# Gate and up projections of a fused attention and gated-MLP layer by seven block products instead of eight

## The chip, the cores and the metric

The kernel runs on one core of one Trainium2 chip. Its time is what the device takes for one launch, in microseconds (us); the three runs of the kernel before took 1195.88 to 1196.09 us, with a median of 1195.92 us. PE is TensorE (matrix products), DVE is VectorE, ACT is ScalarE, POOL is GpSimd, and SP is the engine whose queue issues the DMA transfers.

## The reference

The layer normalises 2 x 1024 tokens of width 512, runs a causal linear attention with 16 heads, adds its normalised output to the input, and then runs a gated MLP whose hidden values are thinned out: of each four neighbours only the two largest in magnitude stay.

```python
x = x + _layernorm(attention(_layernorm(x), Wq, Wk, Wv, Wo))
x = x + _layernorm(ffn(_layernorm(x), w_gate, w_up, w_down))

def ffn(x, w_gate, w_up, w_down):          # x: (2, 1024, 512)
    h = silu(x @ w_gate) * (x @ w_up)      # 512 -> 2048, twice
    h_sparse = _sparsify_2to4(h)           # keep 2 of each 4 neighbours
    return h_sparse @ w_down               # 2048 -> 512
```

Everything is float32. The kernel reaches that precision by splitting each operand into a high part (rounded to the matmul's fp32r type) and a low part (the rest). Each product then takes three matmuls: high x high, low x high, high x low.

## The kernel before

All five engines run programs written out by hand, which meet at semaphores. Each engine works strictly in its own program order. Time is cut into slots. 66 attention slots (`slot_a`, 0 to 65) come first and then 76 MLP slots (`slot_f`, 0 to 75). `TICKS` (L37) gives the common order, and every engine has its own `slot_a` and `slot_f`.

The MLP works on eight units (`UNITS`: two batches times four blocks of 512 hidden values), each with eight slots. A unit has two halves of 512 tokens, and a half has four row blocks (i = 0 to 3) of 128 hidden values, ordered so that the four blocks hold the four neighbours of each group. In slot n PE runs, for one row block and one half of the tokens:

- `gate(n)`: four 128-wide slices of the input (KT = 4), three matmuls each, 12 in all, into a gate bank (`psG`);
- `down(y)`: 12 matmuls of the down projection for 128 tokens of an earlier half;
- `project(psU..)`: 12 matmuls of the up projection into an up bank (`psU`).

Two gate banks and two up banks are used in turn, so that PE fills one while ACT and DVE empty the other. ACT computes silu straight from the gate bank (L1001), DVE multiplies it with the up bank into `hid` (L1255), and ACT writes the magnitudes (L997). After four slots DVE compares pairs (`pair`, L1206), makes the masks and multiplies (`keep_two`, L1212), ACT casts the high parts (L1006) and POOL and DVE subtract to get the low parts (L1401 through the helper at L1339, and L1239). DVE adds each finished `down` bank to `Y` (L1271). DVE also has the statistics of the normalisations (`variance`, L1057, three instructions), POOL the power and the shift (L1344, L1357) and ACT the scaling (L936).

Weights come in pieces of 128 x 512 through a ring of four staging buffers. ACT casts the high part (L891), and POOL subtracts the low part (L1339). A gate or up piece is loaded once per unit and serves both halves, so a unit takes eight such pieces and four pieces of the down weights.

The normalised input of the MLP is turned by PE (`turn`, L601), and split by ACT (`split_x`, L852) and DVE (L1081) into `Xh`, `Xl`, which hold both batches' halves: batch 1 is turned in slots 8 to 22 (`MID_1`, L84), long before slot 32 needs it. The last unit's second half is masked after the last gate product, next to nine remaining `down`s.

Of the kernel before, what the change touches and what calls it, by code (L numbers as in the profile page):

```python
# [7 lines left out]
ALU = mybir.AluOpType  # L8
# [5 lines left out]
P = 128  # L14
B, S, DM = 2, 1024, 512
KVH, REP = 4, 4
W = 512
# [8 lines left out]
LAST = SLOTS - 8  # L26
OPEN = 13
# [21 lines left out]
def down_at(n):  # L49
    y = n - 6 if n < 60 else 54 if n == 61 else n - 9 if n >= SLOTS else -1  # L50
    return y if 0 <= y < SLOTS else None


# [29 lines left out]
MID_0 = [39, 42, 43, 46, 47, 50, 51, 54]  # L83
MID_1 = [8, 10, 12, 14, 16, 18, 20, 22]  # L84


def sum_tick(kind, b, t):
    if kind == "res":
        return tick_a(32 * b + 26 + t)
    return tick_f(65 + t if b else 30 + t)  # L90
# [8 lines left out]
def stat_tick(job):  # L99
    if job[0] in ("res", "out"):  # L100
        return sum_tick(*job)
    return turn_tick(*job) - 2


def norm_tick(job):
    if job[0] in ("res", "out"):
        return sum_tick(*job) + 1
    return turn_tick(*job) - 1
# [18 lines left out]
def weight_plan():  # L127
    plan = [(("q", 0, i), -1) for i in range(4)] + [(("k", 0, 0), -1)]
    plan += [(("v", 0, kk), -1) for kk in range(KT)] + [(("o", 0, h), -1) for h in range(4)]
    for u in range(1, UNITS + 1):  # L130
# [4 lines left out]
        else:  # L135
            plan += [(("g", 0, 0), base - 1), (("g", 0, 1), base)]
        if u > 1:
            plan += [(("o", u - 1, h), base + 1) for h in range(4)]
        if more:
# [4 lines left out]
            if u == NU:  # L144
                plan += [(("v", 1, 2), base + 4), (("v", 1, 3), base + 5)]
    plan += [(("g", 0, 2), 58), (("g", 0, 3), 59), (("u", 0, 0), 60), (("u", 0, 1), 61), (("u", 0, 2), 64),
             (("u", 0, 3), 65)]
    for u in range(UNITS):
        plan += [(("d", u, i), tick_f(8 * u + 1 + i)) for i in range(3)]
        down = [(("d", u, 3), tick_f(8 * u + 5 if u else 4))]  # L150
        if u in (0, UNITS - 1):
            plan += down
        if u + 1 < UNITS:
            for j in range(4):
                plan += [(("g", u + 1, j), tick_f(8 * u + 5 + j)), (("u", u + 1, j), tick_f(8 * u + 5 + j))]
                if j == 0 and u:
                    plan += down
# [7 lines left out]
def by_dve(piece):  # L165
    return piece[0] == "d" and piece[2] == 3


def split_count(k):
    kind = by_dve(PLAN[k][0])  # L170
    return sum(by_dve(piece) == kind for piece, _ in PLAN[:k + 1])


def pieces_at(tick, kinds):
    return [k for k, (piece, when) in enumerate(PLAN) if when == tick and piece[0] in kinds]
# [15 lines left out]
def build(nc, x, wq, wk, wv, wo, wg, wu, wd, cos_t, sin_t, causal, eye, x1, v_rest, out):  # L191
    with ExitStack() as ctx:
        def sb(name, shape, dtype=F32):
            return ctx.enter_context(nc.sbuf_tensor(name, shape, dtype))
# [5 lines left out]
        with ExitStack() as early:  # L200
# [1277 lines left out]
```

## Time and profile before

| | |
|---|---|
| median of three runs | 1195.92 us (1195.88 to 1196.09) |
| profiled execution, first to last instruction | 1194.3 us |
| outside that span (median less span) | 1.6 us |
| PE busy | 1183.0 us, 99% |
| DVE busy | 762.5 us, 64% |
| ACT busy | 497.5 us, 42% |
| POOL busy | 493.6 us, 41% |

The page names no time of its own for the profiled execution beside its span, so the span stands for it. The busy time of an engine is the union of its instructions. PE's matmuls are pipelined: each is shown as some 0.39 us, but a new one starts about every 0.227 us, and that distance, not the shown length, is what a matmul costs. DVE's instructions overlap a little too, so that the distance from one start to the next is again the better measure.

### The profile page before, as it was taken

What the parts mean: (1) busy time and instruction counts of PE and PEld (TensorE: products, weight loads), DVE (VectorE), ACT (ScalarE), POOL (GpSimd) and SP (SyncE); (2) the same over time, 40 slices, a digit from 0 to 9 for tenths busy, and PEclk for the clock granted to TensorE, in tenths of its full rate; (3) what the DMA queues carried; (4) which work ended last, traced back from release to release, by engine and by line L of the source; (5) the groups of instructions that cost most, each with busy time, mean ns of one, the idle gap of its engine ahead of it and who ended that gap; (6) DMA issues with size and microseconds to landing.
All of it is one profiled execution on the core that took longest, in us unless ns stands there. A gap on an engine that the chain in (4) does not pass through costs nothing.

```text
span 1194.3 us, 16009 instructions
## 1 busy us (share of the span) xinstructions
PE 1183.0 (99%) x5958; PEld 998.5 (84%) x5958; DVE 762.5 (64%) x1300; ACT 497.5 (42%) x981; POOL 493.6 (41%) x399
## 2 busy tenths in 40 slices
PE   9999999999999999999999999999999999999997
PEld 7888888888888888888888888888888888888885
DVE  8944756756664456666665476676567765555568
ACT  5534444544544345455355443433333342333322
POOL 6421533515555125244245444443425552334313
PEclk9999999999999999999999999999999999999998
DMA  7221323323534214133143222211103231212111
GB/s 225 80 78 52 102 72 80 89 49 80 146 98 141 58 47 131 47 87 94 30 124 102 97 80 71 71 62 45 62 12 105 97 98 45 62 44 62 45 44 71
DMA packets 58222, 95.03 MB, mean 80 GB/s; under 512 B 6944, under 2 KB 15392, under 8 KB 58144
## 3 DMA queue, kind: packets, MB, share of 16 engines
q1 hardware_dynamic: 58144, 94.01, 27.2%
q8 instruction: 47, 0.77, 0.3%
q14 instruction: 31, 0.25, 0.1%
HBM read 67.24 MB, written 11.53 MB: 66 GB/s over the span
## 4 chain that ended last, share of the span: by engine, by line
PE 95%; DVE 3%; DMA 0%; issue 0%; POOL 0%; ACT 0%; SPq 0%; DVEq 0%
PE bank_q L567 10%; PE bank_q L565 10%; PE bank_q L566 10%; PE bank_y L567 5%; PE bank_y L566 5%; PE bank_y L565 5%; PE bank_od L724 5%; PE bank_od L565 4%; PE bank_od L566 4%; PE bank_od L567 4%; PE bank_od L727 4%; PE bank_t L567 4%; PE bank_t L565 4%; PE bank_t L566 4%; PE bank_s L565 4%; PE bank_s L566 4%
## 5 line engine op out<-in xcount | busy, mean ns | idle before, releaser
L565 PE MATMUL bank_q<-x_hi,w_hi 128*128 128x512 f32 x432 | 172.9, 400 | 0.0
L1339 POOL TENSOR_TENSOR w_lo<-stage,w_hi 128x512 fp32r<-128x512 f32 x80 | 109.3, 1376 | 147.9 <-ACT w_hi L891 147.2
L567 PE MATMUL bank_q<-x_lo,w_hi 128*128 128x512 f32 x432 | 168.9, 391 | 0.0
L566 PE MATMUL bank_q<-x_hi,w_lo 128*128 128x512 f32 x432 | 168.3, 390 | 0.0
L1339 POOL TENSOR_TENSOR big_lo<-hidden,big_hi 128x512 fp32r<-128x512 f32 x30 | 69.0, 2321 | 188.5 <-ACT big_hi L1006 188.5
L1339 POOL TENSOR_TENSOR big_lo<-q_rows,big_hi 128x1024 fp32r<-128x1024 f32 x31 | 74.0, 2386 | 117.2 <-ACT big_hi L930 117.2
L997 ACT ACTIVATE scratch<-hidden 128x512 f32<-128x512 f32 x64 | 40.6, 634 | 176.2 <-DVE hidden L1255 176.2
L567 PE MATMUL bank_y<-wout_lo,a_hi 128*128 128x512 f32 x256 | 100.0, 391 | 0.0
L565 PE MATMUL bank_y<-wout_hi,a_hi 128*128 128x512 f32 x256 | 99.8, 390 | 0.0
L566 PE MATMUL bank_y<-wout_hi,a_lo 128*128 128x512 f32 x256 | 99.8, 390 | 0.0
L567 PEld LDWEIGHTS bank_q<-x_lo,w_hi 128*128 128x128 f32 x432 | 81.1, 188 | 17.6
L724 PE MATMUL bank_od<-v_rows,scratch 128*128 128x130 f32 x512 | 95.2, 275 | 0.0
L566 PEld LDWEIGHTS bank_q<-x_hi,w_lo 128*128 128x128 f32 x432 | 81.3, 188 | 15.4
L565 PEld LDWEIGHTS bank_q<-x_hi,w_hi 128*128 128x128 f32 x432 | 81.2, 188 | 15.3
L959 ACT ACTIVATE scratch<-bank_od,small 128x128 f32<-128x128 f32 x256 | 73.5, 374 | 42.1 <-DVE small L1161 42.1
L727 PE MATMUL bank_od<-st_rows,q_rows 128*128 128x130 f32 x448 | 86.6, 275 | 0.0
L1339 POOL TENSOR_TENSOR wout_lo<-stage,wout_hi 128x512 fp32r<-128x512 f32 x44 | 67.2, 1552 | 42.3 <-ACT wout_hi L891 42.3
L971 ACT CAST a_hi<-bank_s 128x512 fp32r<-128x512 f32 x64 | 37.6, 587 | 111.6 <-PE bank_s L689 111.6
L724 PEld LDWEIGHTS bank_od<-v_rows,scratch 128*128 128x128 f32 x512 | 79.1, 191 | 3.7
L1344 POOL TENSOR_TENSOR small<-small 128x1 f32<-128x1 f32 x64 | 38.0, 593 | 86.4 <-DVE small L1072 85.8
L1271 DVE TENSOR_TENSOR y_acc<-bank_od,y_acc 128x512 f32<-128x512 f32 x42 | 28.8, 685 | 63.7 <-PE bank_od L567 63.7
L727 PEld LDWEIGHTS bank_od<-st_rows,q_rows 128*128 128x128 f32 x448 | 67.5, 190 | 0.0
(333 smaller groups left out, 2987.3 us busy)
## 6 DMA issues: line engine op xcount, KB each, us to landing
q_rows<-scratch SPq DMA_DIRECT2D x116, 128.0 KB, 2.3
x_rows<-x SPq DMA_DIRECT2D x48, 256.0 KB, 2.9
stage<-wq SPq DMA_DIRECT2D x32, 256.0 KB, 2.7
stage<-wo SPq DMA_DIRECT2D x32, 256.0 KB, 2.7
stage<-wg SPq DMA_DIRECT2D x32, 256.0 KB, 2.6
stage<-wu SPq DMA_DIRECT2D x32, 256.0 KB, 2.8
stage<-wd SPq DMA_DIRECT2D x32, 256.0 KB, 2.6
x<-x_rows SPq DMA_DIRECT2D x16, 256.0 KB, 2.4
```

What stands on the lines that cost most here:

```text
L565: pe.matmul(ps, whi, xhi, start=first, stop=False, skip_group_check=True)
L566: pe.matmul(ps, wlo, xhi, start=False, stop=False, skip_group_check=True)
L567: return pe.matmul(ps, whi, xlo, start=False, stop=last, skip_group_check=True)
L724: ins = pe.matmul(o, Sf[:, h * P:(h + 1) * P], Vr[:, c, :], start=True, stop=first, skip_group_check=True)
L727: ins = pe.matmul(o, Q[:, (2 * p + h // 2) % 4, h % 2, t], St[:, :], start=False, stop=True, skip_group_check=True)
L959: act.activation(Tn[:, h * P:(h + 1) * P], sums[:, h // 2, h % 2, 0:P], ACT.Identity, scale=share[:, h:h + 1]).then_inc(act_a, 1)
L971: copy(Ah[:, :, :].rearrange("p h t -> p (h t)"), psS[:, :]).then_inc(act_ah, 1)
L997: act.activation(ab[:, i, :], hid[:, i, :], ACT.Abs).then_inc(act_ab, 1)
L1271: dve.tensor_tensor(Y[:, t, :], down_bank(y), Y[:, t, :], ALU.add).then_inc(dve_yf, 1)
L1339: return pool.tensor_tensor(dst, full, hi.bitcast(F32), ALU.subtract)
L1344: pool.tensor_tensor(rstd[q % 4], mv[q % 4][:, 1:2], mhalf, ALU.pow).then_inc(pool_rs, 1)
```

## The change

Strassen's scheme computes a 2 x 2 block product with seven block products instead of eight. Here the blocks are two row blocks of the weights, two halves of the input width (KT = 4 slices become two and two), and two halves of the tokens. A group of four slots, a quad (`quad_of`), now makes two row blocks for both halves of the tokens, where before it made four row blocks for one half. Its seven products are made for gate and for up, 14 in all of six matmuls each (84 matmuls, where four slots of `gate` and `project` had 96).

- **PE.** The quad's four beats are `products_12`, `products_67`, `products_5`, `products_34`. There is one pair of banks (gX, uX, which collect a running sum) and another (gY, uY). A sum in gX or uX is copied out by ACT before PE adds the next product to it, and DVE adds gY or uY to the copies.
- **Row sums.** ACT: six copies a quad (`keep_sums`) and four silus. DVE: three `gate_sum`, three `up_sum`, four `gated`.
- **Weights.** The products need sums and differences of weight blocks: `combine_weights` on DVE, twice a quad with four instructions of 128 x 256. Seven pieces (`unit`) a quad are split by ACT and POOL, where before it was eight in two quads. They stand in a ring of five. Two of the seven are split as two halves.
- **Input.** For tokens 512 to 1023 of a batch, DVE makes the combinations T1, T2, T3 (`combine_x`, six instructions of 128 x 256) and T4 (`combine_4`, three of 128 x 1024); ACT and POOL split them (`cast_t`, `t_low`, `cast_t4`, `t4_low`). There is room for one batch's combinations alone, so batch 1 is turned in slots 29 to 32 (`MID_1`), split in slots 30 to 33 (`SPLIT_1`), and its T4 is made in slot 34. Batch 0's are made in attention slots 55 to 62.
- **Masks.** Both halves of a unit's tokens are complete only when its second quad is, so the masking comes later (slots 8u + 8 to 8u + 13), and so do the `down`s (`down_beat`). Twelve `down`s stand behind the last product, where nine did.

The core of the diff, with most of the semaphores, buffers and bookkeeping left out:

```diff
+def down_beat(y):
+    if y >= LAST:
+        return y + 9
+    v, j = y // 8, y % 8
+    n = 8 * v + 11 + min(j, 6)
+    if v == 2 and 3 <= j <= 5:
+        return 32
+    return SLOTS if y > 51 else n
-MID_1 = [8, 10, 12, 14, 16, 18, 20, 22]
+MID_1 = [29, 29, 30, 31, 31, 32, 32, 32]
+STAT_1 = [27, 27, 28, 30, 30, 31, 32, 32]
+NORM_1 = [28, 28, 29, 31, 31, 32, 32, 32]
+SPLIT_1 = [30, 30, 31, 32, 32, 32, 33, 33]
+            def product(ps, v, side, of, first):
+                wh, wl = w_hi[:, v % RING, HALVES[side]], w_lo[:, v % RING, HALVES[side]]
+                for kk in range(2):
+                    c = slice(kk * P, kk * P + P)
+                    ins = three(ps, wh[:, c], wl[:, c], of[0][:, kk, :], of[1][:, kk, :], first and kk == 0, kk == 1)
+                return ins
+            def products_12(k):
+                g.wait_ge(dve_xl, 4 * (5 + 2 * b))
...
+                product(gX, v, 0, B11, True).then_inc(pe_g, 1)
...
+                product(gY, v, 1, B21, True).then_inc(pe_g, 1)
...
+                product(uX, v + 1, 0, B11, True).then_inc(pe_u, 1)
...
+                product(uY, v + 1, 1, B21, True).then_inc(pe_u, 1)
+            def products_67(k):
+                g.wait_ge(pool_tl, 4 * (b + 1))
...
+                product(gX, v + 2, 0, T2, False).then_inc(pe_g, 1)
+                g.wait_ge(dve_cg, 3 * k + 1)
+                product(gY, v + 2, 1, T3, True)
...
+            def products_34(k):
...
+                g.wait_ge(act_n, 6 * k + 5)
+                product(gX, v + 5, 0, B22, False).then_inc(pe_g, 1)
+                g.wait_ge(dve_cg, 3 * k + 2)
+                g.wait_ge(pool_t4, b + 1)
+                product(gY, v + 5, 1, T4, False).then_inc(pe_g, 1)
...
+            def keep_sums(k, i):
...
+                copy(gates[(0, 2, 1)[i]], gX).then_inc(act_n, 1)
...
+                copy(hid(u, row, h), uX).then_inc(act_n, 1)
+            def combine_weights(k, up):
...
+                g.wait_ge(pool_w, 7 * k + 3 if up else 7 * k - 1)
+                dve.tensor_tensor(one, c1, c2, ALU.add).then_inc(dve_ss, 1)
+                dve.tensor_tensor(three, a1, c1, ALU.subtract)
+                g.wait_ge(dve_ss, own + 1)
+                dve.tensor_tensor(two, one, a1, ALU.subtract).then_inc(dve_ss, 1)
+                g.wait_ge(dve_ss, own + 2)
+                dve.tensor_tensor(four, a2, two, ALU.subtract).then_inc(dve_ws, 1)
+            def combine_4(b):
...
+                dve.tensor_tensor(to, B21[0].bitcast(F32), T2[0].bitcast(F32), ALU.subtract).then_inc(dve_t4s, 1)
+                dve.tensor_tensor(to, to, B21[1].bitcast(F32), ALU.add).then_inc(dve_t4s, 1)
+                dve.tensor_tensor(to, to, T2[1].bitcast(F32), ALU.subtract).then_inc(dve_t4, 1)
+            def gate_sum(k, i):
...
+                dve.tensor_tensor(to, to, gY, ALU.add).then_inc(dve_cg, 1)
 # DVE, slot_f
+                for t in splits:
+                    if t != 5:
+                        split_x(("mid", 1, t))
+                for job in stats:
+                    if job[0] == "mid":
+                        variance(job)
+                if n < SLOTS and beat == 0:
+                    if u and not second_half:
+                        pair(u - 1, 1, 0)
+                    elif u:
+                        keep_masks(u - 1, 1)
+                    gate_sum(k, 0)
...
+                    up_sum(k, 0)
...
+                    if u and not second_half:
+                        keep_masks(u - 1, 0)
+                if n < SLOTS and beat == 2:
+                    gate_sum(k, 1)
+                    for y in downs:
+                        add_down(y)
+                    up_sum(k, 1)
+                    if k + 1 < QUADS:
+                        combine_weights(k + 1, 0)
+                    if second_half:
+                        pair(u, 0, 0)
+                if n < SLOTS and beat == 3:
+                    gated(k, 1)
+                    for y in downs:
+                        add_down(y)
+                    if u and not second_half:
+                        pair(u - 1, 1, 1)
+                    gate_sum(k, 2)
+                    gated(k, 2)
+                    up_sum(k, 2)
+                    if k + 1 < QUADS:
+                        combine_weights(k + 1, 1)
...
+                if n == 34:
+                    combine_4(1)
+                for w in range(UNITS):
+                    if n == late_piece(w):
+                        split_down(w)
```

## Rows read from the trace of the kernel before

**Rows 1.** The page: busy time, share of the span, instructions.
```profile
PE 1183.0 (99%) x5958; PEld 998.5 (84%) x5958; DVE 762.5 (64%) x1300; ACT 497.5 (42%) x981; POOL 493.6 (41%) x399
```
**Rows 2.** The page: the chain that ended last, by engine.
```profile
PE 95%; DVE 3%; DMA 0%; issue 0%; POOL 0%; ACT 0%; SPq 0%; DVEq 0%
```
**Rows 3.** PE's timeline, slot 1: start us, us, engine, line, operation, tiles.
```profile
669.35 0.39 PE L565 MATMUL bank_q<-x_hi,w_hi 128*128 128x512 f32 x1
...
672.07 0.39 PE L565 MATMUL bank_q<-x_hi,k_hi 128*128 128x512 f32 x1
```
**Rows 4.** DVE's timeline, one half of the tokens in slots 28 to 32.
```profile
909.10 0.69 DVE L1208 TENSOR_TENSOR scratch<-scratch 128x512 bf16<-128x512 f32 x1 [0.70 <-ACT scratch L997]
909.71 0.68 DVE L1209 TENSOR_TENSOR scratch<-scratch 128x512 f32<-128x512 f32 x1
...
911.03 0.69 DVE L1215 TENSOR_TENSOR scratch<-scratch 128x512 bf16<-128x512 f32 x1
...
914.30 0.68 DVE L1227 TENSOR_TENSOR hidden<-hidden,scratch 128x512 f32<-128x512 f32 x1
914.90 0.42 DVE L1229 TENSOR_TENSOR scratch<-scratch 128x512 bf16<-128x512 bf16 x1
915.24 0.42 DVE L1231 TENSOR_TENSOR scratch<-scratch 128x512 bf16<-128x512 bf16 x1
...
917.55 3.33 DVE L1239 TENSOR_TENSOR big_lo<-hidden,big_hi 128x512 fp32r<-128x512 f32 x2
```
**Rows 5.** Groups by line, whole trace: busy us, mean ns, idle before.
```profile
L1239 DVE TENSOR_TENSOR x_lo<-hidden,x_hi 128x512 fp32r<-128x512 f32 x4 | 2.5, 684 | 0.0
L1157 DVE TENSOR_SCALAR small<-bank_od 128x4 f32<-128x4 f32 x64 | 10.0, 157 | 65.4 <-PE bank_od L727 59.8 <-PE bank_od L724 5.5
L1068 DVE BATCH_NORM_STATS2 small<-x_rows 128x6 f32<-128x512 f32 x24 | 16.4, 684 | 0.1
L1321 DVE TENSOR_TENSOR big_lo<-q_rows,big_hi 128x1024 fp32r<-128x1024 f32 x1 | 1.2, 1218 | 0.0
L1344 POOL TENSOR_TENSOR small<-small 128x1 f32<-128x1 f32 x64 | 38.0, 593 | 86.4 <-DVE small L1072 85.8
L1339 POOL TENSOR_TENSOR big_lo<-q_rows,big_hi 128x1024 fp32r<-128x1024 f32 x31 | 74.0, 2386 | 117.2 <-ACT big_hi L930 117.2
```
**Rows 6.** POOL's timeline, slots 22 to 26.
```profile
856.63 1.30 POOL L1339 TENSOR_TENSOR u_lo<-stage,u_hi 128x512 fp32r<-128x512 f32 x1
883.01 4.60 POOL L1339 TENSOR_TENSOR big_lo<-hidden,big_hi 128x512 fp32r<-128x512 f32 x2 [19.14 <-ACT big_hi L1006]
```
**Rows 7.** DVE's and POOL's timelines over the same five microseconds.
```profile
932.92 1.00 DVE L1208 TENSOR_TENSOR scratch<-scratch 128x512 bf16<-128x512 f32 x1
933.85 1.77 DVE L1209 TENSOR_TENSOR scratch<-scratch 128x512 f32<-128x512 f32 x1
933.33 1.74 POOL L1339 TENSOR_TENSOR wout_lo<-stage,wout_hi 128x512 fp32r<-128x512 f32 x1
```
**Rows 8.** ACT's groups, 700 to 1140 us.
```profile
L997 ACT ACTIVATE scratch<-hidden 128x512 f32<-128x512 f32 x54 | 34.2, 634 | 156.5 <-DVE hidden L1255 156.5
L891 ACT CAST w_hi<-stage 128x512 fp32r<-128x512 f32 x32 | 19.0, 613 | 0.0
L936 ACT ACTIVATE x_rows<-x_rows,small 128x512 f32<-128x512 f32 x8 | 6.5, 816 | 4.3 <-POOL small L1357 4.3
```
**Rows 9.** DVE's timeline in attention slot 61.
```profile
641.48 0.69 DVE L1189 TENSOR_TENSOR y_acc<-bank_y,y_acc 128x512 f32<-128x512 f32 x1 [2.06 <-PE bank_y L567]
```
**Rows 10.** The end: DVE's timeline, and the granted clock by windows (PEclk after the busy times).
```profile
1161.23 0.69 DVE L1255 TENSOR_TENSOR hidden<-bank_t,scratch 128x512 f32<-128x512 f32 x1 [2.95 <-PE bank_t L567]
1186.04 0.68 DVE L1271 TENSOR_TENSOR y_acc<-bank_od,y_acc 128x512 f32<-128x512 f32 x1
1187.00:1188.00 1.00, 0.00 (x0) 0.00 (x0) 0.90 (x4) 0.94 (x2) 0.80 (x3) 1.00 0.66 248
1188.00:1189.00 1.00, 0.00 (x0) 0.00 (x0) 1.00 (x3) 0.69 (x1) 0.78 (x1) 0.62 0.00 0
```

More of the change, by code:

```diff
@@ L26 @@
 LAST = SLOTS - 8
+QUADS = SLOTS // 4
+RING = 5
 OPEN = 13
@@ L941, in slot_a @@
                 m = s - 1
+                late = []
                 if s % 4:
@@ new lines, in slot_f @@
+                for job in norms:
+                    if job[0] == "mid":
+                        normalise(job)
+                if n < SLOTS and beat == 0:
+                    if not second_half and u:
+                        absolute(u - 1, 1, 0)
+                    keep_sums(k, 0)
+                    silu(k, 0)
+                    if 5 in splits:
+                        split_x(("mid", 1, 5))
+                    unit(7 * k + 5)
+                    unit(7 * k + 6)
+                    if second_half:
+                        absolute(u, 0, 1)
@@ L1083, in split_x @@
                 half, t = halves(*job), job[2] % 4
+                if job[0] == "mid" and job[2] > 3:
+                    combine_x(job)
+                    return
+                if job[0] == "mid":
+                    half = 0
                 g.wait_ge(act_xh, k + 1)
@@ new lines, in slot_a, with pair @@
+                if s == 61:
+                    combine_4(0)
+                if s == 62:
+                    combine_weights(0, 1)
+            def pair(u, i, h):
+                low, high, c = (least_23, most_23, c23) if i else (least[h], most[h], c01[h])
+                r = pair_number(u, i, h)
+                g.wait_ge(act_ab, r + 1)
+                dve.tensor_tensor(c, low, second, ALU.is_ge)
+                dve.tensor_tensor(high, low, second, ALU.max)
+                dve.tensor_tensor(low, low, second, ALU.min).then_inc(dve_pr, 1)
@@ L1272, in slot_f @@
-                for job in at(tick, stat_tick, LATER + ENDING):
-                    variance(job)
-                for k in pieces_at(tick, "d"):
-                    if by_dve(PLAN[k][0]):
-                        split(k)
+                k, beat = quad_of(n)
+                u, second_half = k // 2, k % 2
+                splits = [t for t in range(TT) if SPLIT_1[t] == n]
+                downs = [y for y in range(SLOTS) if add_beat(y) == n]
+                stats = at(tick, stat_tick, LATER + ENDING)
```

763 lines of the change are left out of this document (544 added, 219 removed).

## The prediction

> **What bounds the kernel now.** First the busy times: PE is busy for 99% of the span, DVE for 64%, the others for 41 to 42% [rows 1]. Then the chain that ended last: 95% of it is PE [rows 2]. So a matmul taken away is worth its whole distance to the next one, as long as PE is kept fed. That distance is in PE's timeline: twelve matmuls lie between 669.35 and 672.07 us, 0.227 us each [rows 3]. What the change loads instead is DVE, and DVE's own pace is read from starts. A 128x512 fp32 instruction follows the one before it after 0.60 us (909.10 to 909.71), a bf16 one after 0.34 (914.90 to 915.24), and the mask work from L1215 up to the first product takes 3.3 us, with the two bf16 instructions behind it 4.0 [rows 4]. A low part costs 0.68 us alone [rows 5], but two of them take 3.33 us while POOL works on its own low parts [rows 4, 6].
>
> **What the change takes away.** Four slots had 96 gate and up matmuls, a quad has 84. Over 16 quads 192 are gone: 192 x 0.227 = 43.5 us. Downs, turns and the attention keep their counts. If nothing else moved, the span would be 1194.3 - 43.5 = 1150.8.
>
> **What it adds in a steady pair of quads.** PE now needs 264 x 0.227 = 59.8 us for two quads (65.4 before). DVE, at 0.60 an instruction and 0.33 for one of 128x256 (my estimate, halfway from a 128x4 one at 0.16 to the 0.60; bounds 0.16 and 0.60) [rows 4, 5]: 12 sums and 8 products 12.0, pairs 12 x 0.60 = 7.2, masks 2 x 4.0 = 8.0, masked products 4.8, low parts 2.4 undisturbed, 8 downs 4.8, sixteen half-wide weight combinations 5.3, one weight split 0.6. That is 45.1 of 59.8 us, 75%; before it was 32.6 of 65.4. So on average PE still sets the pace. But DVE's work is one queue, and PE's next product waits at fixed places in it.
>
> I walked two quads beat by beat with these numbers, PE's beats being 36, 48, 12, 36, 36, 36, 24 and 36 matmuls. ACT copies (0.61 each [rows 8]) and sums come in time nearly everywhere: a bank filled in one beat is wanted again a beat later, some 5 us on. The weak place is the short third beat (12 matmuls, 2.7 us, no down) of a unit. There DVE has the sum, two downs, the sum, `combine_weights` and then `split_down`, which waits for ACT; and ACT gets to it only after three weight units, two magnitudes and two casts (about 4 us at 0.61 to 0.63 [rows 8]). Behind the waiting split stand `gated`, `pair` and the third `gate_sum`. That sum ends about 10 us after the fourth beat began, while PE wants it 9.5 us after (36 + 6 matmuls): 0.4 us late undisturbed, 3 us with the disturbance below. I take 2 us at each of six such places, 12 us (bounds 2 and 24). A seventh lies in the batch change.
>
> **The shared disturbance.** When POOL subtracts from SBUF, DVE's two-input instructions from SBUF stretch: L1209 took 1.77 us, not 0.68, while POOL's own took 1.74, not 1.30 [rows 4, 6, 7]. The two take turns. POOL's steady load rises from 15 subtractions in two quads (8 + 4 + 3) to 21 (14 + 4 + 3), DVE's two-input work from SBUF from about 23 to 32 us. The Trainium skill has this as a rule (SBUF — State Buffer, "SBUF: two separate sides"): the port pair that VectorE and GpSimd share is an exclusive lock for a whole instruction. The trace agrees, with 1.77 and 1.74 us for the two that met. What it would make of the time is the second rival.
>
> **Batch 0's combinations (attention slots 55 to 62).** Added on DVE: four `combine_x` (6 x 0.33 and three short waits, 2.3 us each), one `combine_4` (3 x 1.22 = 3.7 us), two weight combinations (1.3 each). A slot there has about 2 us of idle DVE before it takes PE's output [rows 9], which hides most; `combine_4` alone exceeds it, and two `combine_x` meet in slots 55 and 59. I take 4 us (0 to 10, the sum of 15.5 less six slots' idle, is the outer bound).
>
> **Batch 1's combinations (slots 28 to 35).** Before, the turning lay in slots 8 to 22, far ahead. Now three things come one after another with little for PE to do.
> 1. `products_12(8)` needs the low part of tile 3. Up to there DVE has in slots 30 to 32 three `variance`s at 1.1 (0.68 for the first of their three instructions [rows 5], the two short ones make up the rest: my estimate), four splits of 0.6, seven sums and products 4.2, a down 0.6, a pair 1.8 and two combinations 2.7, 15 us, behind a backlog of some 2.5 (tiles 0 to 2 have their `variance`s in slots 27 and 28), with about 2 us of waits for POOL and ACT. PE has 12 + 24 matmuls and the turns, 9.5 us. ACT's normalisation of tiles 3 and 4 (0.82 each) waits for POOL, which stands behind the unit that waits for DVE's combination. PE starts 10 us late (7 to 11).
> 2. `products_67(8)` needs the T's of tile 7. From the start of slot 32 PE has 24 matmuls, three turns and three downs, 15 us. DVE has a `combine_x`, two `variance`s, a wait for POOL's scalings and ACT's normalisations and magnitudes, a pair, two sums, a `combine_x`, two downs, the masks (4.0) and two more `combine_x`: 23 us, then 1 for ACT and 2 for POOL (1.30 and half of it). PE waits 9.5 us (7 to 13).
> 3. `products_34(8)` needs T4. Its chain starts with the end of the first half of `products_5(8)`: copy 0.8, sum 0.6, two downs 1.2, sum 0.6, weights 1.3, `combine_4` 3.7, ACT about 1.1, POOL 2.4 [rows 5, 8], hand-overs 0.6: 12.3 us. PE has 12 matmuls, 2.7 us. It waits 9.5 us (8 to 12).
> Together 29 us (22 to 36). This is the largest cost, and nothing hides it: PE's program has no other work between these points.
>
> **The clock.** At the end the granted clock was still 1.00 in 1187 to 1188 and 0.62 in 1188 to 1189, with PE's last matmul near 1186 [rows 10]. So it falls to its lower level, 1.2 GHz, some 2 us after work stops. After each of the three long waits PE would begin at half speed. No row shows how long; if it is as long as the fall took, 2 us at half speed lose 1 us. I take 3 us for three waits (0 to 12).
>
> **Results of batch 0 (slots 36 to 43)** add DVE's `variance` (1.1) and POOL's scalings (0.6 and more [rows 5]) and additions to these fuller beats: 3 us (0 to 8).
>
> **The end.** Before, the last product's result came at 1161.2 and the last down's at 1186.0: nine downs (24.5 us) without a gap [rows 10]. Now both halves of the last unit wait for the last product. Four older downs cover 10.9 us; the first masked half needs sum and product 1.5, magnitudes 1.4, pair 1.9, down 0.6, masks 4.0, down 0.6, first product 0.6, ACT 0.8 and POOL up to 2.3, 13.5 us, and the second low part 2 more. PE waits 4.5 us, and about 2.5 for the second half: 7 us (4 to 11).
>
> **Sum.** 1194.3 - 43.5 + 12 (steady) + 4 (attention) + 29 (batch change) + 3 (clock) + 3 (results) + 7 (end) = 1208.8 of span. The median stands 1.6 us above the span, so I forecast 1210.4 us, 1.2% slower. The 58 us of new waits come from bounds of 28 and 101; I trust the middle, since most terms are chains with named instructions.
>
> **Rivals.**
> - *The seams are short (faster).* The mechanism: DVE reaches the batch change with no backlog and 128x256 instructions cost nearer 0.2 than 0.33, so that the chains in 1 and 2 shrink to 6 us each; T4's wait of 8 stays, the steady places cost 2, the end 5, the attention 1. That is 28, and 2 for the clock, against 43.5: 1182 us. For it: DVE is at 75%, and PE never waited in the trace of before. Against it: the work in slots 30 to 33 is counted instruction by instruction. It decides as soon as the waits are under 43.5 us. Chance 0.33.
> - *The pair of engines is the bound (slower still).* If the two engines take turns without exception, as in [rows 7], DVE's 32 us of two-input work and POOL's 21 subtractions at 1.30 (27 us, [rows 6]) fill 59 of the 59.8 us of two quads. Every wait of one for a semaphore is then lost to PE as well; at some 4 us for each of seven pairs of quads (about the 3.5 us by which the two low parts of [rows 4] and POOL's pair of [rows 6] stretch together) that is 28 us beyond the forecast, 1238 us. This is what the Trainium skill's rule (SBUF — State Buffer, "SBUF: two separate sides") would lead to. Against it: in 883.01 to 887.61 POOL did two of 1.3 us while DVE did some 3 us of its own [rows 4, 6], so about a tenth overlaps. Chance 0.14.
> - *It doesn't do what it says:* PE waits as much as it saves and the time stays at 1196. Chance 0.04.
>
> **How the numbers follow.** The forecast (1198.5 to 1222) has 0.49. The range over the cases is 1174 to 1238: it leaves out a tenth on either side. A measurement of this kernel tells 0.2% (2.4 us) from no change. Faster by more than that 0.33, within it 0.04, slower by more 0.63.
>
> **What would show it.** PE: 5766 matmuls (5958 - 192), at 0.227 us where it is fed. PE idle in slots 31 to 35 of the MLP in three gaps of about 10 us, the first ended by DVE's `split_x`, the others by POOL's `t_low` and `t4_low`; the granted clock under 1.00 behind them. DVE busy above 80% of the MLP's span, POOL above 55%. Gaps of a few us at the start of every other quad, ended by `gate_sum`. I am wrong if the MLP shows PE without gaps in slots 28 to 35, or if the gaps before T4 are under 5 us.

## The result, and the profile after

The changed kernel takes 1323.36 us (median of four runs, 1322.28 to 1324.45) against 1196.01 (1195.88 to 1196.15) for the kernel before in the same comparison. The ratio is 1.1065 with an interval of 1.1049 to 1.108. The forecast was 1210.4 with a range of 1174 to 1238: the side is right, the size is far off.

The page of the changed kernel, busy times and three rows of the forty slices, and the chain that ended last:

```profile
PE 1190.7 (90%) x5766; PEld 984.8 (75%) x5766; DVE 985.2 (75%) x1568; ACT 580.9 (44%) x1175; POOL 599.8 (45%) x499
...
PE   9999999999999999999788798987666888998886
...
DVE  8745766666655566667747898997877879898998
...
PEclk9999999999999999999999999998778998999998
...
PE 55%; DVE 29%; issue 6%; ACT 5%; POOL 4%; DMA 0%; DVEq 0%; SPq 0%; ACTq 0%
```

PE has its 192 matmuls fewer (5958 before, [rows 1]), and yet its share falls from 99 to 90% and its part of the chain from 95% [rows 2] to 55%. DVE has 29% of the chain. The two engines' rows show two kinds of loss: PE at 8 and 9 through most of the MLP, and a hole at the batch change.

The waits of PE from the MLP's first sum to the end (line, what it waited for, us in total, times, longest):

```profile
PE bank_t L652 <- DVE scratch L1591: 21.3, 16, 2.2
PE bank_q L652 <- ACT scratch L1189: 15.1, 6, 4.7
PE bank_od L652 <- POOL wout_lo L1775: 12.5, 5, 2.6
PE bank_t L652 <- POOL x_lo L1775: 12.3, 1, 12.3
PE bank_q L652 <- POOL x_lo L1775: 11.8, 1, 11.8
PE bank_od L652 <- DVE y_acc L1619: 7.6, 4, 2.8
```

`gate_sum` (L1591), at the start of the quads, is the largest. The two long waits, for the low parts of T1 to T3 and of T4, stand where they were forecast.

The table splits the loss by stage. A unit runs from its first `gate_sum` to the next unit's. "PE needs" is the count of its matmuls at 2.72 / 12 = 0.227 us (a turn of four short ones at 0.44). "Lost" is the length less that need. The first and last rows are measured against the kernel before. The first `gate_sum` comes at 677.8 us, and PE of the kernel before had done as many matmuls in time for a sum at 658.7. From there on the last unit has 384 matmuls, which with the work behind them take 95.6 us at the pace of the kernel before. The last two columns are two of the experiments below (11 and 14).

| stage | PE needs | length after | lost after | lost, POOL thin | lost, all thin |
|---|---|---|---|---|---|
| attention's end | | | 19.1 | 16.0 | 3.6 |
| unit 0 | 41.0 | 56.2 | 15.2 | 9.2 | 7.3 |
| unit 1 | 51.7 | 67.0 | 15.3 | 3.3 | -0.1 |
| unit 2 | 59.8 | 70.2 | 10.4 | 1.3 | 0.3 |
| unit 3 (turning of batch 1) | 56.6 | 87.5 | 30.9 | 20.7 | 17.4 |
| unit 4 (T's of batch 1) | 66.6 | 105.1 | 38.5 | 28.2 | 14.9 |
| unit 5 | 59.8 | 77.9 | 18.1 | 5.5 | 2.2 |
| unit 6 | 59.8 | 70.2 | 10.4 | 1.2 | 0.3 |
| unit 7 and the end | 95.6 | 108.5 | 12.9 | 2.9 | 3.7 |
| sum | | | 170.8 | 88.3 | 49.6 |

The spans differ by 1320.5 - 1194.3 = 126.2 us, and with the 43.5 saved 169.7 are lost. The rows add up to 1.1 us more, since the matmuls of the kernel before are not exactly 0.2267 us apart in the MLP either (0.2274). The most telling row is unit 2, which has no turning and no statistics, only the steady work: 70.2 us, where the kernel before took 65.4.

What DVE does there is in the timelines. First DVE, then POOL, in a stretch of attention slot 60 where both work on weights:

```profile
641.78 0.42 DVE L1411 TENSOR_TENSOR w_sums<-stage 128x256 f32<-128x256 f32 x1
642.11 1.52 DVE L1412 TENSOR_TENSOR w_sums<-stage 128x256 f32<-128x256 f32 x1
643.55 1.51 DVE L1414 TENSOR_TENSOR w_sums<-w_sums,stage 128x256 f32<-128x256 f32 x1
645.09 1.37 DVE L1416 TENSOR_TENSOR w_sums<-stage,w_sums 128x256 f32<-128x256 f32 x1
```
```profile
641.95 2.83 POOL L1775 TENSOR_TENSOR w_lo<-stage,w_hi 128x512 fp32r<-128x512 f32 x2 [1.92 <-ACT w_hi L1043]
644.74 1.45 POOL L1799 TENSOR_TENSOR x_rows<-x_rows,y_acc 128x512 f32<-128x512 f32 x1
```

The first combination starts before POOL does and takes 0.42 us. The next starts 0.33 us behind it, which is what the prediction estimated. By then POOL has begun, and each further one takes 1.37 to 1.52 us, the length of one POOL instruction: the last two end at 645.06 and 646.46, 0.3 us after POOL's subtractions end at 644.78 and 646.19. Four cost 4.6 us, not 1.3.

### The profile page after: what moved, and what is told of

Read it like the earlier page. It is cut to its first block, busy times and chain, and to the rows that moved or that the text cites. A ratio compares the mean times of both kernels' runs of the same rounds, so it can differ in the third digit from the quotient of the medians.

```text
span 1320.5 us, 16350 instructions
## 1 busy us (share of the span) xinstructions
PE 1190.7 (90%) x5766; PEld 984.8 (75%) x5766; DVE 985.2 (75%) x1568; ACT 580.9 (44%) x1175; POOL 599.8 (45%) x499
## 4 chain that ended last, share of the span: by engine, by line
PE 55%; DVE 29%; issue 6%; ACT 5%; POOL 4%; DMA 0%; DVEq 0%; SPq 0%; ACTq 0%
PE bank_q L652 6%; PE bank_q L654 6%; PE bank_q L653 6%; PE bank_y L654 4%; PE bank_y L652 4%; PE bank_y L653 4%; PE bank_od L869 4%; PE bank_od L872 3%; PE bank_t L652 2%; PE bank_s L776 2%; PE bank_t L654 2%; PE bank_t L653 2%; DVE w_sums L1412 2%; DVE w_sums L1414 2%; DVE scratch L1591 2%
## 5 line engine op out<-in xcount | busy, mean ns | idle before, releaser
L652 PE MATMUL bank_q<-x_hi,w_hi 128*128 128x512 f32 x496 | 206.1, 416 | 39.4 <-ACT scratch L1189 15.1
L653 PE MATMUL bank_q<-x_hi,w_lo 128*128 128x512 f32 x496 | 198.8, 401 | 0.0
L654 PE MATMUL bank_q<-x_lo,w_hi 128*128 128x512 f32 x496 | 198.8, 401 | 0.0
L1775 POOL TENSOR_TENSOR w_lo<-stage,w_hi 128x512 fp32r<-128x512 f32 (+1 forms) x104 | 131.2, 1272 | 138.5 <-ACT w_hi L1069 87.3
L1775 POOL TENSOR_TENSOR w_lo<-w_sums,w_hi 128x512 fp32r<-128x512 f32 (+1 forms) x80 | 100.5, 1264 | 186.0 <-ACT w_hi L1046 121.6
L652 PE MATMUL bank_t<-x_hi,w_hi 128*128 128x512 f32 x160 | 68.3, 427 | 33.5 <-DVE scratch L1591 21.3
L652 PE MATMUL bank_od<-wout_hi,big_hi 128*128 128x512 f32 x176 | 72.0, 409 | 14.9 <-POOL wout_lo L1775 12.5
L1182 ACT ACTIVATE scratch<-scratch 128x512 f32<-128x512 f32 x48 | 30.4, 633 | 117.6 <-DVE scratch L1591 117.6
L1775 POOL TENSOR_TENSOR big_lo<-hid_a,big_hi 128x512 fp32r<-128x512 f32 x32 | 53.3, 1686 | 61.9 <-ACT big_hi L1213 61.9
L653 PE MATMUL bank_od<-wout_hi,big_lo 128*128 128x512 f32 x176 | 70.8, 403 | 0.0
```

The lines of the kernel that those rows point to most:

```text
L652: pe.matmul(ps, whi, xhi, start=first, stop=False, skip_group_check=True)
L653: pe.matmul(ps, wlo, xhi, start=False, stop=False, skip_group_check=True)
L654: return pe.matmul(ps, whi, xlo, start=False, stop=last, skip_group_check=True)
L1182: act.activation(gates[(0, 1, 0, 2)[i]], gates[(0, 1, 0, 2)[i]], ACT.Silu).then_inc(act_s, 1)
L1775: return pool.tensor_tensor(dst, full, hi.bitcast(F32), ALU.subtract)
```

## The experiments

Each ran once beside the kernel before, which took 1195.8 to 1196.5 us; the ratio of the result above is the only one with an interval. Among these runs the moment at which the MLP's first sum starts falls into two groups, 676.4 to 678.4 us (after and runs 7, 8 and 13) and 672.5 to 674.7 (the others, but for 6 and 14, in which work before it is made narrow), even where two programs are the same up to there. So 4 to 5 us of a total can be this and not the edit.

The traces show how it comes about. Near 634 us PE has waited 2.86 us for POOL, in every run but 6 and 14. Behind the same wait the granted clock over 634 to 636 us was 0.50 in the changed kernel and 1.00 in run 5:

```profile
634.00:636.00 2.00, 2.00 (x5) 1.63 (x6) 1.94 (x6) 1.09 (x3) 2.00 (x3) 0.50 0.01 4
```
```profile
634.00:636.00 2.00, 1.82 (x8) 1.57 (x9) 1.97 (x6) 0.94 (x3) 2.00 (x3) 1.00 0.00 0
```

The eleven distances between the next twelve matmuls take 4.0 us there and 2.6 here. DVE's sum comes later by that, and so do the weight combinations shown above. They then start only 0.17 us before POOL's first subtraction and take until 646.47. In run 5 they were done before POOL began:

```profile
641.92 0.42 DVE L1416 TENSOR_TENSOR w_sums<-stage,w_sums 128x256 f32<-128x256 f32 x1
645.58 0.69 DVE L1518 TENSOR_TENSOR y_acc<-bank_y,y_acc 128x512 f32<-128x512 f32 x1 [2.03 <-PE bank_y L654]
642.18 2.57 POOL L1775 TENSOR_TENSOR w_lo<-stage,w_hi 128x512 fp32r<-128x512 f32 x2 [1.92 <-ACT w_hi L1043]
```

All runs fit: the eleven distances took 3.7 to 4.8 us in the changed kernel and in runs 2, 7, 8, 11 and 13 and 2.6 in runs 3, 4, 5, 9, 10 and 12, and of the first group only runs 2 and 11, in which POOL's weight subtractions are narrow, still begin the MLP early. Why the clock fell behind this wait in some runs and not in others is open.

Where an effect is small, the lengths of the units are compared, which agree within 0.6 us, mostly 0.1, where nothing was changed.

**1. The saving alone: the kernel before with 192 matmuls left out.** One slice of `project` (3 matmuls of 24 in a slot) is left out.

```diff
-                    project(psU[n % 2], 4 + j, half).then_inc(pe_u, 1)
+                    for kk in range(KT - 1):
+                        ...
+                        ins = three(psU[n % 2], Wh[4 + j][:, c], Wl[4 + j][:, c], Xh[:, half, kk, :], Xl[:, half, kk, :],
+                                    kk == 0, kk == KT - 2)
+                    ins.then_inc(pe_u, 1)
```

> The kernel before with the last of four input slices left out of the up projection: 3 of 24 gate and up matmuls a slot, 192 in all, and nothing else changed. This is the change's saving alone. If PE is the bound as the profile of before says, the time falls by 43.5 us to 1152.4 (1150 to 1156). If DVE or POOL stood close behind PE, less: 1165 or more.

Measured: 1152.42 us, span 1150.6. The saving of 43.5 us is exact, and nothing of the kernel before stood in its way.

**2. POOL's low parts of the gate and up weights made narrow.**

```diff
-                    lo(lo_to, of, hi_to).then_inc(pool_w, 1)
+                    lo(lo_to[:, narrow], of[:, narrow], hi_to[:, narrow]).then_inc(pool_w, 1)
```

> The changed kernel with POOL's low parts of the gate and up weights (unit) narrowed to 16 of 512 columns (the rest of those low parts is left out); every other instruction stays. In the changed kernel a unit of eight slots lasts 70.2 us, where PE has 59.8 us of matmuls. Theory 1 (DVE and POOL take turns at SBUF): without these reads DVE's two-input instructions go back to 0.34 to 0.6 us each, a unit lasts 60 to 63 us, and the time falls by 60 to 80 us to about 1250. Theory 2 (DVE's program with its fixed places is too long whatever POOL does): a unit stays at 69 to 70 us and the time above 1310.

Measured: 1250.26 us; unit 2 61.3 us instead of 70.2. PE and DVE have every instruction they had. This run alone can't tell whether DVE was stretched by POOL's reading or PE waited for a late POOL; the next one can.

**3. POOL as busy as before, but writing only.** Three memsets of 0.53 us stand in place of each subtraction, so these low parts are left out.

```diff
-                    lo(lo_to, of, hi_to).then_inc(pool_w, 1)
+                for i in range(2):
+                    pool.memset(lo_to.bitcast(F32), 0.0).then_inc(pool_ms, 1)
+                    g.wait_ge(pool_ms, 2 * v + i + 1)
+                pool.memset(lo_to.bitcast(F32), 0.0).then_inc(pool_w, 1)
```

> As the run before, but in place of each of POOL's low parts of the gate and up weights stand three memsets of the same 512 columns, which only write (these low parts are left out). POOL stays about as busy. Theory 1a (what meets is POOL's reading of SBUF with DVE's second input): a unit lasts 60 to 63 us, as without them. Theory 1b (any POOL access stops DVE): a unit stays near 70 us. Theory 3 (POOL is simply late with its weights, and that holds PE): also near 70 us.

Measured: 1266.82 us, unit 2 62.1 us. The windows over unit 2, first of the changed kernel, then of this run (PE, PEld, DVE, ACT, POOL busy, granted clock):

```profile
801.10:871.30 70.20, 64.01 (x273) 51.51 (x272) 63.38 (x90) 30.17 (x58) 33.75 (x25) 0.98 0.14 46
```
```profile
785.80:847.90 62.10, 60.33 (x267) 49.64 (x266) 53.52 (x91) 30.00 (x58) 33.51 (x49) 1.00 0.16 51
```

POOL is busy for 33.5 us (33.8 in the changed kernel), and DVE with the same work is busy for 53.5 instead of 63.4. So what stretches DVE is not that POOL is busy, nor that it writes: it is POOL reading from SBUF. But the whole kernel gets back less than in run 2: its span is 1265.0, against 1248.5 there and 1320.5 in the changed kernel. Of the 72.0 us that run 2 gives, 55.5 go with the reading, and 16.5 come back when POOL is as busy as before, mostly in units 0, 3 and 4 (3.7, 4.4 and 2.7 us longer than in run 2). That part fits a POOL that is late with its results.

**4. DVE's weight combinations made narrow.**

```diff
                 g.wait_ge(pool_w, 7 * k + 3 if up else 7 * k - 1)
+                if k:
+                    one, two, three, four, a1, a2, c1, c2 = [t[:, 0:16] for t in (one, two, three, four, a1, a2, c1, c2)]
```

> The changed kernel with DVE's weight combinations narrowed to 16 of 256 columns from the second quad on (so most of the combined weights is stale). They take 2.7 us of DVE a quad in the changed kernel. Theory 1: they are the instructions that wait longest for POOL (0.91 and 0.73 us where one alone takes 0.42), but sixteen short ones still wait for POOL's turns, so a unit goes from 70.2 to 63 to 67 us. Theory 2: DVE's program gets 16 x 0.26 = 4 us shorter and a unit lasts 66 us. The run sizes this part; it doesn't tell the two apart.

Measured: 1292.79 us, unit 2 66.3 us. It gives 3.9 us a unit; POOL's narrow weights gave 8.9.

**5. T4 of batch 1 in slot 33.** `combine_4(1)`, its cast and its low part move from slot 34 to slot 33, on all three engines.

```diff
-                if n == 34:
-                    combine_4(1)
...
                     for y in downs:
                         add_down(y)
+                    if n == 33:
+                        combine_4(1)
```

> Batch 1's T4 (combine_4, its cast and its low part) is made in slot 33 instead of 34; nothing is left out. If the wait before T4 (12.3 us in the trace of after) is the chain that the prediction walked, most of it goes and the kernel comes out about 10 us shorter than after, 1313 us. If DVE simply has more work there than time, the wait moves to the next product and the time stays within 3 us, 1320 to 1323 us.

Measured: 1310.24 us. Unit 4 is 96.9 us long instead of 105.1, no other changes by more than 0.6; the other 4.5 us are the earlier entry into the MLP. The wait of 12.3 us for T4 is gone. So the wait was the chain that the prediction walked, behind which there was 8.2 us of slack to win, not the whole of it.

**6. The activations' combinations made narrow**, in both batches.

```diff
-                dve.tensor_tensor(one, first, B11[0][:, :, c].bitcast(F32), ALU.subtract).then_inc(dve_ts, 1)
+                few = slice(t * P, t * P + 8)
+                ...
+                dve.tensor_tensor(one, first, B11[0][:, :, few].bitcast(F32), ALU.subtract).then_inc(dve_ts, 1)
```

> The activations' combinations are cut to a sixteenth or a quarter of their columns in both batches (T1, T2, T3 8 of 128, T4 32 of 256; the rest of them is left out): instructions and waits stay, their durations go. It prices what the combinations cost on all engines. If the seams (attention's end, batch change) are slow because of them, some 8 us of the 20 at attention's end and 20 of the 70 us lost in the two units around the batch change come back: 1295 us. If these units are slow because DVE has a backlog from masks, statistics and weights, 10 us come back in all: 1313 us.

Measured: 1297.05 us. 12.2 us come back before the MLP's first sum (up to 5 of them the scatter above), 12.8 in unit 4, 0.7 in unit 3. The T's of batch 1 are made in slots 32 to 34, which belong to unit 4; unit 3 has none and is slow for other reasons.

**7. Work moved off POOL: the low parts of the first two weight blocks on DVE.**

```diff
+            def weight_low(v):
+                if on_dve(v):
+                    ...
+                    g.wait_ge(act_w, v + 1)
+                    dve.tensor_tensor(w_lo[:, v % RING, :], of, w_hi[:, v % RING, :].bitcast(F32),
+                                      ALU.subtract).then_inc(dve_w, 1)
...
                         combine_weights(k + 1, 0)
+                        for v in range(7 * k + 7, 7 * k + 10):
+                            weight_low(v)
```

> From quad 1 on, DVE and not POOL subtracts for the low parts of the first two weight blocks of a quad (30 instructions); nothing is left out. Taking turns at SBUF: 30 x 1.3 us of POOL's turns go and 30 x 0.6 of DVE's come, 39 - 18 = 21 us less, 1302 us. If instead the length of DVE's own queue decides, and POOL's work beside it costs little, DVE's 18 us more lengthen the units: 1341 us.

Measured: 1298.74 us, unit 2 66.6 us. More work for the busier engine makes the kernel 25 us faster. Of all runs this one tells the two theories apart most cleanly, since nothing is left out and they differ in sign.

**8. The same for five of the seven blocks.**

> As the run before, with the first five of a quad's seven weight blocks (75 instructions) on DVE. Taking turns: 75 x 1.3 less 75 x 0.6, 52 us less, 1271 us, or some 10 us worse than that because DVE now waits for ACT's casts as well. The length of DVE's queue: 45 us more, 1368 us.

Measured: 1297.04 us, unit 2 66.8 us: 26 us short of what taking turns alone would give, 16 short of the expectation with its allowance for ACT's casts, and no better than two blocks. DVE's waits from 700 to 880 us, with two blocks and then with five:

```profile
DVE scratch L1563 <- ACT scratch L1214: 8.3, 7, 1.7
```
```profile
DVE scratch L1563 <- ACT scratch L1214: 5.4, 5, 1.6
DVE w_lo L1433 <- ACT w_hi L1055: 4.5, 6, 0.7
```

DVE now waits for ACT's casts too, and its queue is full (busy for 93.0 of the 100 us from 805). So the yield ends where DVE has no room left.

**9. All four low parts of the hidden activations on DVE.** `hidden_lows` on DVE runs over four row blocks and POOL's is gone.

```diff
-                for i in range(2, 4):
+                for i in range(4):
                     g.wait_ge(act_hh, 4 * d + i + 1)
```

> DVE makes all four low parts of the hidden activations, POOL none of them (32 instructions move); nothing is left out. Taking turns: POOL's 32 x 1.3 go, DVE's 32 x 0.6 come: 22 us less, 1301 us. If the length of DVE's own queue decides (the masks stand in it just before, and it waits here for ACT's casts at 0.82): 19 us more, 1342 us.

Measured: 1305.86 us, of which 5.0 us the earlier entry; unit 2 69.0 us instead of 70.2. The sign is that of taking turns, the yield half: here DVE takes on 2.4 us a unit next to the masks, its fullest place.

**10. The wait at the MLP's start.** The copy of the first up product waits for the last attention product only.

```diff
                 g.wait_ge(pe_pv, SLOTS)
-                g.wait_ge(pe_y, 4 * SLOTS)
+                if row > 1:
+                    g.wait_ge(pe_y, 4 * SLOTS)
```

> The first up product's copy and product (into hid_a, which lies where the queries lay) no longer wait for the last attention output, only for the last attention product; the rows of hid_b keep that wait. Nothing is left out. In the trace of after ACT stood 6.26 us at that copy, and with it everything behind it in ACT's order up to the copy that ends PE's 3.30 us at 691.90. If ACT's order is the cause, about 3 us go: 1320 us. If POOL's scaling, which stands behind the weights' low parts, is what PE waits for anyway, nothing goes: 1323 us.

Measured: 1313.97 us; unit 0 is 52.5 us long instead of 56.2. So 3.7 us were ACT's order; the remaining 4.3 us less came before the first `gate_sum` and belong to the scatter.

**11. All of POOL's low parts for gate, up and hidden made narrow.**

```diff
-                    lo(hidden(d)[1][:, i, :], hid(d // 2, i, d % 2), hidden(d)[0][:, i, :]).then_inc(pool_hl, 1)
+                    few = slice(0, 16)
+                    lo(hidden(d)[1][:, i, few], hid(d // 2, i, d % 2)[:, few],
+                       hidden(d)[0][:, i, few]).then_inc(pool_hl, 1)
```

> POOL's low parts of gate and up weights and of the hidden activations are cut to 16 of 512 columns (the rest is left out); its three for the down weights stay. It shows DVE almost undisturbed. Taking turns: the rest of the stretching goes beyond the first thin run (1250 us): a unit at PE's own 59.8 us, the kernel at some 1232 us, DVE's work in a unit near the 45 us that the prediction counted. If the low parts of the hidden activations never cost anything, 1248 us.

Measured: 1239.70 us, unit 2 61.1 us. The groups by line from 800 to 870 us (busy us, mean ns), first of the changed kernel, then of this run:

```profile
L1578 DVE TENSOR_TENSOR big_lo<-hid_b,big_hi 128x512 fp32r<-128x512 f32 x4 | 5.9, 1505 | 0.0
...
L1591 DVE TENSOR_TENSOR scratch<-scratch,bank_t 128x512 f32<-128x512 f32 x6 | 4.0, 672 | 0.0
L1412 DVE TENSOR_TENSOR w_sums<-stage 128x256 f32<-128x256 f32 x4 | 3.8, 958 | 0.0
```
```profile
L1591 DVE TENSOR_TENSOR scratch<-scratch,bank_t 128x512 f32<-128x512 f32 x7 | 4.7, 678 | 4.7 <-ACT scratch L1189 4.7
...
L1578 DVE TENSOR_TENSOR big_lo<-hid_b,big_hi 128x512 fp32r<-128x512 f32 x4 | 2.6, 690 | 0.7 <-ACT big_hi L1213 0.6
...
L1412 DVE TENSOR_TENSOR w_sums<-stage 128x256 f32<-128x256 f32 x4 | 1.7, 422 | 0.0
```

Instructions with both operands in SBUF are slow beside POOL (1505 and 958 ns) and quick without it (690 and 422). The sum with one operand in PSUM (L1591) takes 0.67 us in both. DVE's busy time in unit 2 is now 48.9 us.

**12. Spare matmuls in the two long waits of batch 1.** They are written into the banks that hold quad 8's sums in progress, not into free ones as the expectation says, so the sums of that quad are left out.

```diff
+                if k == 8:
+                    g.wait_ge(act_n, 6 * k + 1)
+                    fill(gX, 44)
                 g.wait_ge(pool_tl, 4 * (b + 1))
```

> Spare matmuls (44 and 48 of 128x512, 10 and 11 us, into banks that are free then) fill the two long waits of batch 1, before T2's and before T4's product; nothing is left out, nothing else moves. In the trace of after the matmuls behind these waits lie 0.43 us apart for some 18 of them, not 0.227. If the clock costs what its slow matmuls take longer, 18 x 0.2 = 3.6 us go in these two units: 1319 us. If DVE sets the pace there and the slow matmuls hide behind it, the time stays: 1323 us.

Measured: 1314.18 us; unit 4 is 101.5 us long instead of 105.1, all others within 0.1 (the rest is the entry, 4.7). PE's timeline behind the wait for T1 to T3, without and with the spare matmuls:

```profile
979.21 0.80 PE L652 MATMUL bank_q<-x_hi,w_hi 128*128 128x512 f32 x1 [11.83 <-POOL x_lo L1775]
979.80 0.63 PE L653 MATMUL bank_q<-x_hi,w_lo 128*128 128x512 f32 x1
980.23 0.63 PE L654 MATMUL bank_q<-x_lo,w_hi 128*128 128x512 f32 x1
```
```profile
974.65 0.50 PE L652 MATMUL bank_q<-x_hi,w_hi 128*128 128x512 f32 x1 [2.04 <-POOL x_lo L1785]
974.99 0.39 PE L653 MATMUL bank_q<-x_hi,w_lo 128*128 128x512 f32 x1
975.22 0.40 PE L654 MATMUL bank_q<-x_lo,w_hi 128*128 128x512 f32 x1
```

The granted clock over the 60 us around the two waits (965 to 1025, and 960 to 1020):

```profile
965.00:1025.00 60.00, 35.91 (x139) 28.71 (x138) 45.01 (x66) 15.30 (x29) 23.83 (x16) 0.80 0.10 33
```
```profile
960.00:1020.00 60.00, 56.56 (x248) 46.17 (x247) 48.34 (x73) 18.61 (x36) 26.32 (x20) 1.00 0.11 35
```

It rises from 0.80 to 1.00. Behind an idle PE the matmuls start 0.43 us apart, behind a working one 0.23. The 3.6 us were expected from 18 slow matmuls and came.

**13. The four cures that leave nothing out, together** (5, 7, 9 and 10).

> T4 of batch 1 a slot earlier, the first two weight blocks and all hidden activations on DVE, the start's wait shortened; nothing is left out. If these gains add up, 13 + 25 + 3 + 22 us less than after, 1260 us; if they take away the same collisions, or DVE's queue gets full (49.2 us of 59.8 by the prediction's counting), 1275 to 1285 us. In no case under the 1196 us of before.

Measured: 1272.23 us, unit 2 65.0 us, unit 4 91.3. The gains do not quite add up. This is the fastest complete version of the changed kernel that was tried, and still 76 us slower than the kernel before.

**14. All the added arithmetic narrow at once** (4, 6 and 11).

> POOL's low parts of gate, up and hidden, the activations' combinations and the weight combinations are all cut to a few columns (the rest of them is left out); every instruction and wait stays. It shows what is left of the loss when the added arithmetic is nearly free. If amounts of work cost the time, alone and by taking turns, most of the rest goes: 1239.7 less 22 for the activations, less 10 to 30 for the weights, 1190 to 1208 us, and the floor is the 1152 us of the run with fewer matmuls. If order, hand-overs and the place of the turning cost it, it stays above 1215 us.

Measured: 1201.01 us, span 1199.2, within the 1190 to 1208 of "amounts of work". Its waits of PE from 840 to 1000 us:

```profile
PE bank_q L652 <- POOL x_lo L1780: 4.3, 1, 4.3
PE bank_q L652 <- POOL w_lo L1780: 4.0, 1, 4.0
PE bank_t L652 <- POOL x_lo L1780: 3.3, 1, 3.3
PE bank_s L705 <- ACT x_rows L1114: 3.0, 1, 3.0
PE bank_t L652 <- DVE scratch L1596: 3.0, 2, 2.0
```

Even with nearly free combinations the kernel does not get below the one before. What is left is 48.4 us over the floor of 1150.8, 32 us of it in units 3 and 4. The waits shown say that it is mostly the order: turning, statistics, scaling, splitting and combining follow one another with little for PE to do between. About 8 of the 32 us are matmuls at a low clock behind these waits, and POOL's down weights and the splits of the input were not made narrow, so how much is order alone was not measured.

## Why the prediction was wrong

Together the runs divide the loss: 169.7 us = 82.6 that go with POOL's low parts (1320.5 - 1237.9) + 38.7 that go when the combinations of weights and activations are narrow too (1237.9 - 1199.2) + 48.4 that remain, put down to order and hand-overs. The first part is not all reading: for the gate and up weights run 3 puts 55.5 us down to reading and 16.5 to a late POOL. It also holds slow clock that went with the waits, and the split depends on the order in which things are made thin, since narrow combinations meet POOL less.

- **The saving, 43.5 us:** right, to 0.1 us.
- **The steady pairs, 12 us (2 to 24): this is the step that failed.** Two us a unit were forecast and 10.4 measured (units 2 and 6). The prediction summed DVE's durations undisturbed (45.1 us; run 11 shows 48.9 busy), set them against PE's 59.8, found 75% and concluded that "on average PE still sets the pace". The disturbance it had read in [rows 7] was then charged at one place a unit. That place was right: behind the third `gate_sum` PE waited 2.2 us. But when DVE comes to an instruction with two operands in SBUF while POOL reads, it waits for POOL's instruction to end, wherever that happens, and the wait stands in the same queue as all its other work. In unit 2 this made DVE's busy time 63.4 us instead of 48.9, and with 6.8 us of its own waits that is the 70.2 of the unit. A sum that shows this beforehand, worked out here after the runs, is DVE's queue plus POOL's subtractions, as if nothing ran side by side: 45.1 + 21 x 1.30 = 72.4 us against PE's 59.8. For the kernel before it is 32.6 + 15 x 1.30 = 52.1 against 65.4, which fits that its PE never waited although the same collisions were there.
- The sum is an estimate, and a coarse one: with the 48.9 us measured for DVE it would be 76.2, since DVE's instructions on PSUM can run beside POOL's. With 45.1 it comes within 3 us of the experiments. Unit 2 by the sum and as measured: two blocks moved 47.5 + 17 x 1.30 = 69.6 and 66.6; five moved 51.1 + 11 x 1.30 = 65.4 and 66.8; hidden moved 69.6 and 69.0; all cures 49.9 + 13 x 1.30 = 66.8 and 65.0; narrow weights on POOL under PE's 59.8, and 61.3.
- **The second rival** (the pair of engines is the bound, 0.14, 1238 us) had the right mechanism and the wrong sum. It compared only DVE's two-input work, 32 us, plus POOL's 27 with PE's 59.8, and so found the pair just full. It left out the 13 us that DVE spends on PSUM and one-input instructions in the same queue. With them the sum would have been 72.4 - 59.8 = 12.6 us over in each unit, 88 us for seven. Its argument against itself was misread too: 2.6 us of POOL and 3 of DVE in 4.6 us overlap by 1 us, a fifth of the stretch and not a tenth. The Trainium skill's rule (SBUF — State Buffer, "SBUF: two separate sides"), an exclusive lock of the shared port pair for a whole instruction, agrees with the rows of 642.11 to 645.09. The rule names DVE instructions with two SBUF inputs, and for them only a GpSimd instruction that reads SBUF. The trace agrees there too: the PSUM sum kept its 0.67 us, and with POOL's memsets in run 3 the combinations took 0.41.
- **Attention's end, 4 us (0 to 10):** 19.1, of which 3.6 are left when the arithmetic is narrow. The instructions were counted rightly; each of the short combinations took up to a whole POOL instruction, 4.6 us for a `combine_weights` that was forecast at 1.3.
- **The MLP's start** was not in the prediction: ACT stood 6.26 us at a copy that waits for the last attention output. Behind it came a table load, the weights and a scaling that waited 3.48 us more for POOL. 3.7 us were ACT's order, by run 10.
- **The batch change, 29 us (22 to 36):** the three waits were found in their places, by their releasers, at 5.3 + 3.9, 11.8 and 12.3 us for 10, 9.5 and 9.5. Together that is 33 us. But units 3 and 4 lose 69.4, and less twice the steady 10.4 that is 48.6. With POOL's gate, up and hidden low parts narrow (run 11) they still lose 48.9 in all, 46.3 without the steady part of 1.3 a unit, so the rest hardly depends on those; 17 us of the 69.4 are matmuls that start 0.3 us or more after the one before, at a low clock. Run 5 confirms the chain of T4, and run 6 prices the T's at 12.8 us of unit 4.
- **The clock, 3 us (0 to 12):** mis-sized. Between 600 and 1320 us 140 matmuls start 0.42 or 0.43 us after their predecessor, 28 us in all, because PE now idles in many places and not in three. Even a wait of 2.86 us had the clock at 0.50 behind it in some runs. For the two waits of run 12 it is 3.6 us, fully on the path. What it costs elsewhere, where DVE sets the pace, was not measured; [rows 10] told only that the clock falls, not how much comes after.
- **Results of batch 0, 3 us (0 to 8):** unit 5 lost 18.1, 7.7 more than a steady one, at the upper bound. With POOL narrow it is 4.3 more.
- **The end, 7 us (4 to 11):** from the first of the twelve `down`s behind the last product to the last matmul it took 43.8 us, where 143 distances need 32.4: 11.3 us, just past its upper bound. With POOL narrow it was 36.2, so 3.8 us are the order of masks and `down`s that was counted, and the rest went with POOL's low parts.
- "The seams are short" (0.33) was wrong throughout, and so was the ground for it: DVE at 75%.
- Of the signs named beforehand, the gaps of slots 31 to 35 were found, and DVE was busy for 84% of the MLP's span (above 80 forecast), but POOL only for 49 (above 55 forecast).

What stays open: why the clock fell behind the wait near 634 us in some runs alone, how the 28 us of slow matmuls divide between path and cover, and how much of the last 48.4 us is order alone.

## What to carry to other kernels

Before moving arithmetic from PE to DVE, add up one steady period as DVE's whole queue plus every POOL instruction that reads SBUF, and compare that with PE's need. Here the kernel before stood at 52 of 65 us by this sum and never waited, the changed one at 72 of 60 and took 70. Where it is more, taking work off POOL helps even if the busier DVE must do it, as long as DVE's own queue has room. And a second batch that must be turned, normalised and combined in one place costs a chain of hand-overs: 32 us were lost there even with the added arithmetic narrow.

## What the runs showed of the hardware

- A 128x256 subtraction on DVE takes 0.42 us alone (0.33 to the next start) and 1.37 to 1.52 beside a reading POOL, 3.3 to 3.6 times as long; a 128x512 one went from 0.69 to 1.5 on average (run 11's rows), 2.2 times.
- POOL's memsets, 0.53 us each and in all as long as its subtractions (POOL busy for 33.5 and 33.8 us in unit 2), left DVE's combinations at 0.41 us and cost a unit 0.8 us against a narrow POOL (62.1 and 61.3).
- DVE's 128x512 sums with one operand in PSUM took 0.66 to 0.70 us in the MLP of every run, beside POOL or not.
- Behind PE's wait of 11.8 us matmuls started 0.43 us apart at first, against 0.227 in a running PE; 10 us of spare matmuls in the wait removed it. Behind a wait of 2.86 us both happened: a granted clock of 0.50 in some runs and of 1.00 in others.
- Such a difference can grow: 1.4 us of slow matmuls shifted four DVE combinations into POOL's subtractions, and the MLP began 4 to 5 us later.
